# Four edits to a fused graph-Mamba-and-experts kernel: another DMA queue, larger clearing pieces, other PSUM banks, another spread of products

## The reference

```python
x = x + gnn(layernorm(x), adj)            # graph step, then a Mamba block
x = x + ffn(layernorm(x))                 # 8 experts, the best one per token

# gnn:
h = layernorm(relu(adj @ x @ gcn_w + gcn_b)) * ln_g + ln_b
xc, z = h @ w_in                          # 256 + 256
u = silu(conv4(xc)); dt = softplus((u @ w_xp)[:8] @ w_dt + b_dt); B, C = (u @ w_xp)[8:]
state_t = exp(dt * A) * state_(t-1) + dt * B_t * u_t      # 16 states per channel, over all tokens
y = (state_t . C_t + u * D) * silu(z);  out = y @ w_out
# ffn:
H = gelu(x @ W1 + b1);  p = softmax(H @ Wg + bg);  e = argmax(p)
out = p[e] * (H @ Wd[e] + bd[e])
```

## Time and profile before

| | |
|---|---|
| time of three runs, us | 1833.7, 1842.24, 1849.21; median 1842.24 |
| the profiled execution, us | 1857.62 |
| its span from first to last instruction, us | 1855.8 |
| busy, us (share of the span) | TensorE 1534.2 (83%), VectorE 1535.7 (83%), ScalarE 877.1 (47%), GpSimd 874.5 (47%) |
| mean granted TensorE clock | 0.902 of 2.4 GHz |
| DMA | 479.42 MB, mean 258 GB/s; SyncE's queue holds 16 engines 70.7% of the span |

### The profile page before, as it was taken

The page is one execution under the profiler, slowest core; times in us unless marked ns, Lnnn a source line. Parts: engine busy times, 40 slices in busy tenths (PEclk is TensorE's granted clock), DMA queues, the critical chain, the costliest instruction groups (busy, mean ns, idle before and its releaser), DMA issues. The chain is left out here.

```text
span 1855.8 us, 16772 instructions
## 1 busy us (share of the span) xinstructions
PE 1534.2 (83%) x4572; PEld 763.5 (41%) x4572; DVE 1535.7 (83%) x2015; ACT 877.1 (47%) x1558; POOL 874.5 (47%) x466
## 2 busy tenths in 40 slices
PE   6998888887989989898989888998989793633676
PEld 2433343333434545354544444443535341422444
DVE  8058898797899998989899989889999988898621
ACT  3134363452636464554646373646465554634311
POOL 0013333444345464645555554646464645557721
PEclk9999998999998999989999989899999996655788
DMA  8788999999897887879697868688787864333320
GB/s 306 252 299 308 307 337 306 338 317 324 305 329 264 307 294 262 282 255 317 246 322 257 311 233 309 248 307 286 283 299 266 309 215 170 101 124 136 120 70 12
DMA packets 164640, 479.42 MB, mean 258 GB/s; under 512 B 19780, under 2 KB 50512, under 8 KB 164418
## 3 DMA queue, kind: packets, MB, share of 16 engines
q1 hardware_dynamic: 155074, 453.31, 70.7%
q0 software_dynamic: 8320, 20.86, 3.5%
q10 hardware_dynamic: 1152, 4.19, 0.6%
HBM read 448.20 MB, written 33.22 MB: 259 GB/s over the span
## 5 line engine op out<-in xcount | busy, mean ns | idle before, releaser
L1162 PE MATMUL ps_adj<-ring,nodes 128*128 128x512 f32 x2048 | 957.6, 616 | 89.4 <-DMA ring<-adj 66.3
L496 POOL TENSOR_TENSOR h_c<-hidden,bc_ring 128x1024 f32<-128x1024 f32 x256 | 601.0, 2348 | 866.4 <-DVE inject L1030 603.2
L957 DVE TENSOR_TENSOR_SCAN hidden<-decay,state,inject 128x512 f32<-128x512 f32 x512 | 627.6, 1268 | 79.5 <-ACT decay L585 54.1
L1162 PEld LDWEIGHTS ps_adj<-ring,nodes 128*128 128x128 f32 x2048 | 397.0, 198 | 612.0 <-issue 480.2
L1030 DVE TENSOR_TENSOR inject<-dtu_sb,bc_ring 128x1024 f32<-128x1024 f32 x256 | 314.6, 1229 | 55.3 <-DMA bc_ring<-bc_dram 35.1
L585 ACT ACTIVATE decay<-dt_sb,negA 128x512 f32<-128x512 f32 x512 | 340.1, 714 | 8.8 <-DVE dt_sb L984 8.6
L1000 DVE TENSOR_TENSOR y_sum<-y_sum,h_c 128x1024 f32<-128x1024 f32 x224 | 273.8, 1222 | 23.9 <-POOL h_c L496 20.8
L578 ACT COPY state<-hidden 128x2 f32<-128x2 f32 x255 | 49.3, 193 | 473.3 <-DVE hidden L957 471.0
L460 POOL DMA_INDIRECT out<-o_sb,out_at x68 | 92.0, 1354 | 71.6 <-DVE o_sb L862 58.7
L455 POOL DMA_INDIRECT bins<-rec,dest x60 | 87.3, 1455 | 10.8 <-issue 10.2
L450 POOL DMA_INDIRECT got<-bins,row_at x60 | 85.0, 1416 | 14.6 <-issue 11.5
(11 more groups left out here) (201 smaller groups left out, 1387.0 us busy)
## 6 DMA issues: line engine op xcount, KB each, us to landing
ring<-adj SPq DMA_DIRECT2D x512, 512.0 KB
bc_ring<-bc_dram SPq DMA_DIRECT2D x256, 512.0 KB, 5.8
wd_ring<-wd_rows SPq DMA_DIRECT2D x64, 320.0 KB
bins<-nodes SPq DMA_DIRECT2D x128, 129.0 KB, 7.8
nodes<-x_rows ACTq DMA_DIRECT2D x8, 512.0 KB, 12.2
x_tile<-x_rows SPq DMA_DIRECT2D x16, 256.0 KB
wd_rows<-Wd SPq DMA_DIRECT2D x8, 256.0 KB
ring<-Wd SPq DMA_DIRECT2D x1, 2048.0 KB, 7.5
```

The source lines that it names most:

```text
L496: nc.gpsimd.tensor_tensor(h_c[:, s % 2], hidden[:, s % 2], over_halves(bc_ring[:, s % BC_RING, 1]), ALU.mult).then_inc(hc_ready, 1)
L957: scan = nc.vector.tensor_tensor_scan(hidden[:, s % 2, h], decay[:, s % 2, h], inject[:, h], state[:, h, s:s + 1], ALU.mult, ALU.add)
L1162: last = nc.tensor.matmul(ps_adj[:, 0], nodes[:, m], ring[:, g % RING, m % GROUP], start=(m == 0), stop=(m == J - 1))
```

## The change

Four parts. (1) The store of the B and C rows and their loads go from SyncE to ScalarE: the store right behind the copy in slot f[9], the loads at the end of each slot, for the state two slots ahead. (2) The bins are cleared in 32 pieces of 4128 bytes on each of 128 partitions instead of 128 pieces of 1032. (3) The W1 products go to both banks of `ps_e`, `ps_y` and bank 1 of `ps_f`, and GELU takes the `ps_f` bank first; the front's waits for GELU change with it. (4) From body 3 on, as far as `MAIN` has no row, the 32 groups of a tile are spread over the slots by `SHARE` instead of two in each.

```diff
+EVEN = (2,) * SLOTS
+SHARE = (3, 3, 2, 3, 2, 2, 2, 1, 2, 2, 0, 3, 2, 3, 0, 2)
+MAIN = {-2: EVEN, -1: (0, 1, 1, 0, 0, 1, 0, 0, 5, 1, 0, 1, 1, 1, 1, 0),
...
-    FILLS = SPACE // P
-    AREAS = 4
+    AREAS, PARTS = 4, 8
...
-            return (ps_f[:, 0], ps_f[:, 1], ps_y[:, 0], ps_e[:, 0])[k]
+            return (ps_e[:, 0], ps_e[:, 1], ps_y[:, 0], ps_f[:, 1])[k]
...
-                counts = table.get(i, () if table is LEAD else (2,) * SLOTS)
+                counts = table.get(i, () if table is LEAD else SHARE)
...
             def clear_bins(n):
-                sp.dma_start(bins.ap()[n * P:(n + 1) * P], nodes[:].rearrange("p j d -> p (j d)")[:, 0:REC]
-                             ).then_inc(zero_in[n * AREAS // FILLS], 16)
+                area, part = n // PARTS, n % PARTS
+                size = SPACE // AREAS
+                width = size * REC // P // PARTS
+                cells_of = bins.ap()[area * size:(area + 1) * size].rearrange("(p n) c -> p (n c)", p=P)
+                sp.dma_start(cells_of[:, part * width:(part + 1) * width],
+                             nodes[:].rearrange("p j d -> p (j d)")[:, 0:width]).then_inc(zero_in[area], 16)
...
                     if i in (1, 2, 3):
-                        for n in range(3 * (SLOTS * (i - 1) + s), min(3 * (SLOTS * (i - 1) + s + 1), FILLS)):
+                        k = SLOTS * (i - 1) + s
+                        for n in range(AREAS * PARTS * k // (3 * SLOTS), AREAS * PARTS * (k + 1) // (3 * SLOTS)):
                             clear_bins(n)
...
-                    if s == min(f[9] + 2, SLOTS - 1) and front:
-                        sp.dma_start(bc_dram.ap()[q].rearrange("s h n -> h s n"), rows_sb[:]
-                                     ).wait_op(rows_ready, c.value(rows_ready, 1, 1), "sem-ge").then_inc(rows_out, 16)
-                    for d, t in next_state(s, mamba, front):
-
-                        freed = c.value(hc_ready, d, t - BC_RING + 1)
-                        if t == 0:
-                            c.wait(rows_out, d, 16)
-                        dma = sp.dma_start(bc_ring[:, t % BC_RING],
-                                           bc_dram.ap()[p if d == 0 else q, t:t + 1].broadcast_to([P, 2, T]))
...
         @block.scalar
+                def fetch_rows(s):
+                    for d, t in ((0, s + 2), (1, s + 2 - SLOTS)):
+                        if (mamba if d == 0 else front) and 0 <= t < SLOTS:
+                            if t == 0:
+                                c.wait(rows_out, d, 16)
+                            c.wait(hc_ready, d, t - BC_RING + 1)
+                            act.dma_start(bc_ring[:, t % BC_RING],
+                                          bc_dram.ap()[p if d == 0 else q, t:t + 1].broadcast_to([P, 2, T])
+                                          ).then_inc(bc_in[t % BC_RING], 16)
...
-                        for k in range(4):
-                            c.wait(h_done, -1, k + 1)
+                        c.wait(h_done, -1, 4)
+                        for k in (3, 0, 1, 2):
                             nc.scalar.activation(H[:, k], h_bank(k), ACT.Gelu, bias=vec("b1", k)
...
+                        c.wait(rows_ready, 1, 1)
+                        act.dma_start(bc_dram.ap()[q].rearrange("s h n -> h s n"), rows_sb[:]).then_inc(rows_out, 16)
...
                     if not (s in (8, 11, 13) or fast and s == 5):
                         exp_decay(s)
+                    fetch_rows(s)
...
         @block.tensor
                         c.wait(xt_ready, -1, 1)
-                        c.wait(xz_ready, 1 if front else 0, 4 if front else 0)
                         c.wait(bh_ready, -5, 4)
+                        c.wait(o_ready, -5, PICKS + 1)
                         for k in range(4):
+                            if k == 3:
+                                c.wait(xz_ready, 1 if front else 0, 4 if front else 0)
                             product(h_bank(k), [(w1_sb[:, k], xn_cols)]).then_inc(h_done, 1)
                     if front and s == f[8]:
                         c.wait(u_ready, 1, 1)
-                        if ffn:
-                            c.wait(h_ready, -1, 1)
...
                         c.wait(low_ready, 1, 1)
                         if ffn:
-                            c.wait(h_ready, -1, 2)
+                            c.wait(h_ready, -1, 1)
```

More of the change, by code:

```diff
@@ L18 @@
 OUT_SLOTS = (0, 10, 11, 12)
-MAIN = {-1: (0, 1, 1, 0, 0, 1, 0, 0, 5, 1, 0, 1, 1, 1, 1, 0),
+EVEN = (2,) * SLOTS
+SHARE = (3, 3, 2, 3, 2, 2, 2, 1, 2, 2, 0, 3, 2, 3, 0, 2)
+MAIN = {-2: EVEN, -1: (0, 1, 1, 0, 0, 1, 0, 0, 5, 1, 0, 1, 1, 1, 1, 0),
         0: (0, 0, 0, 0, 0, 0, 1, 2, 2, 2, 3, 2, 2, 3, 3, 3),
@@ L371, in body @@
                 q = 1 - p
-                f = FRONT.get(i, range(SLOTS))
                 if i == TILES - 2:
@@ L396, in body @@
                         load_experts(wd_ring[:, p], p, wd_in[p])
-                    if s == min(f[9] + 2, SLOTS - 1) and front:
-                        sp.dma_start(bc_dram.ap()[q].rearrange("s h n -> h s n"), rows_sb[:]
-                                     ).wait_op(rows_ready, c.value(rows_ready, 1, 1), "sem-ge").then_inc(rows_out, 16)
-                    for d, t in next_state(s, mamba, front):
-                        freed = c.value(hc_ready, d, t - BC_RING + 1)
-                        if t == 0:
-                            c.wait(rows_out, d, 16)
-                        dma = sp.dma_start(bc_ring[:, t % BC_RING],
-                                           bc_dram.ap()[p if d == 0 else q, t:t + 1].broadcast_to([P, 2, T]))
-                        if freed is not None:
-                            dma.wait_op(hc_ready, freed, "sem-ge")
-                        dma.then_inc(bc_in[t % BC_RING], 16)
                     if s == SLOTS - 1 and mamba:
@@ L472, in body @@
                         if i - 2 < AREAS:
-                            pool.wait_ge(zero_in[i - 2], 16 * FILLS // AREAS)
+                            pool.wait_ge(zero_in[i - 2], 16 * PARTS)
                         c.wait(dest_step, -2, 6)
@@ L479, in body @@
                         for n in range(AREAS):
-                            pool.wait_ge(zero_in[n], 16 * FILLS // AREAS)
+                            pool.wait_ge(zero_in[n], 16 * PARTS)
                         c.wait(ctrl_step, -4, 13)
```

## The result

The changed kernel takes 1833.97 us, the median of 12 runs (1819.1 to 1843.5), against 1844.02 us for the kernel before in the same rounds. The ratio is 0.994, with a 95% interval of 0.9913 to 0.9968: a gain of about 0.6%, where 1.5% was forecast. The profiled execution took 1837.63 us.

What follows compares the result with a forecast made beforehand. VectorE's idle waits were taken as what can be won, VectorE and TensorE having little room. Terms of -8 (tiles 4 to 13), -15 (tiles 0 to 3) and -4 (tile 14) sum to -27 us: ratio 0.985, 1815 us, range 1775 to 1858.

Steps and rivals of the forecast that it cites:

- Tiles 4 to 13, -8 us: New VectorE waits of 3.2 us a tile replace 4.0 at slot 13: -0.8 us in each of ten tiles.
- the row of state 10: VectorE's wait for slot 10's B row, issued 3.5 us ahead: L - 3.5, so 1.2 us a tile.
- the row of state 13: VectorE's wait for slot 13's B row: L - 3.9 + d, so 2.0 us a tile.
- The decay behind that row: Slot 13's decay on ScalarE would end before `inject` is over; still being last would show the forecast wrong.
- d: In tiles 4 to 13, how late the batch's hidden products reach ScalarE's slot 11: taken as 1.2 us, between 0 and 4.4.
- L: Time from issue to landing of a row load on ScalarE's queue: taken as 4.7 us, between 3.6 and 5.7.
- Rival 1: The other queue makes no difference: L stays 5.7, 5.2 us of waits a tile, 1839 us; chance 0.20.
- Rival 2: TensorE stays at 1.2 GHz from `low_sb` on and L is 5.7: 8.4 us a tile, 1871 us; chance 0.15.
- Rival 4: Batch products come no earlier; slot 13's scan starts at 913.5 instead of 910.5; 1853 us; chance 0.06.
- Tiles 0 to 3, -15 us: Larger pieces save 4 us each in tiles 1 and 2, 3 in tile 3; tile 0 saves 4.
- Tile 14, -4 us: The 3.9 us wait for a B row behind the `Wd` load on the same queue goes; at worst 0.
- The banks at nothing: Moving the W1 products removes TensorE's 3.49 us wait for GELU at slot 8, but by itself gives the end nothing.

Runs made afterwards that it cites:

- second profile: The kernel before, unchanged, run again for another profile: 1847.4 us, ratio 1.0008; that profiled execution took 1845.8 us.
- x_fill: The changed kernel with four products of no use (3.6 us at full clock) added in slot 10 before the second `dt` product: 1839.8 us, ratio 0.9969.
- u_queue: The changed kernel with the store and loads of the B/C rows back on SyncE: 1878.0 us, ratio 1.0194.
- u_pieces: The changed kernel with the bins cleared in 128 small pieces again: 1842.7 us, ratio 0.9982.
- u_banks: The changed kernel with the four W1 products in their old banks, with the old waits for GELU: 1836.9 us, ratio 0.9962.
- u_share: The changed kernel with two adjacency groups in every slot again: 1849.2 us, ratio 1.0036.
- the swap alone: The changed kernel with the batch's hidden products 0 and 1 ahead of the logits in slot 10 on TensorE: 1829.4 us, ratio 0.9899.
- the early loads alone: The changed kernel with rows loaded at the slot's head, not its end, in slots 8, 11 and 13: 1839.3 us, ratio 0.9942.
- the three together: The changed kernel with hidden products before slot 10's logits, row loads at the head of slots 8, 11, 13, and two groups per slot: 1815.4 us, 0.9822.

## Why the prediction was off

The time lies in the range, and tiles 1 to 3 and 14 gave what they were to give or more; but the gain is 10 us by the medians, where the sum had 27. The profile after is 20 us below the first profile and 8 us below the second. Of the 17 us that are missing, 10 lie in the base (last below), 5 in tiles 4 to 13 and 3 in the start; the other tiles gave 1 us more than forecast.

*Tiles 4 to 13, -8 us: the step that failed.* The sum was 3.2 us of new waits a tile against 4.0. The new waits are 3.7; the old ones were 3.5 by the second profile. Of the sum's terms, the row of state 10 costs nothing where 1.2 was forecast, and the row of state 13 costs 1.7 where it was 2.0. The decay behind that row, which the prediction had ending in time, costs 0.75 (that it is still last was a sign of being wrong), and the rows of states 15, 14 and 11, which were not in the sum, 1.3.

The term that was mis-sized is d, by which the batch's products come too late. It was taken as 1.2 us, with 4.4 named for the case that the whole stretch runs at 1.2 GHz. It is ScalarE's wait in slot 11: 5.44 us in tile 7 and 4.2 in the mean of nine tiles. In tile 7 the whole stretch from the transposes on is at 1.2 GHz, which costs about 4 us (`x_fill`), and the wait for the gathered rows `got`, 1.14 us, which the prediction did not see, comes on top. The row of tile 14 had shown what an empty stretch does to the logits; I applied it to the logits and to one product, not to what stands before and behind them.

Two other terms erred the other way and hid part of this. L was taken as 4.7 us; from issue to `inject` at state 13 it is 3.4 to 3.9 in the eight tiles that wait for this row, 3.6 in the mean (888.19 to 891.78 in tile 7). That is not the queue's doing. In these tiles the last adjacency load goes out 15 to 20 us before the row, because TensorE frees no place in the ring, and the DMA engines are nearly idle (a share of 0.10 at the most in the two us before the row). In tile 7 (DMA share and GB/s last):

```profile
886.20:888.20 2.00, 2.00 (x4) 0.93 (x3) 1.93 (x3) 1.66 (x2) 1.83 (x2) 0.50 0.00 0
```

So the 3.6 us are those of SyncE's loads with little beside them. Where adjacency is under way, a load on ScalarE's queue takes no less time than one on SyncE's. State 15's rows in tile 7, on SyncE, ScalarE (the first of the two issues) and VectorE:

```profile
890.47 10.63 SPq L383 DMA_DIRECT2D ring<-adj  x6
...
899.06 0.89 ACTq L588 DMA_DIRECT2D bc_ring<-bc_dram  x2
...
904.75 1.23 DVE L1036 TENSOR_TENSOR inject<-dtu_sb,bc_ring 128x1024 f32<-128x1024 f32 x1 [0.68 <-DMA bc_ring<-bc_dram]
```

These are 5.7 us, and 5.1 to 7.0 in the seven tiles that wait there (up to 8.0 at states 11 and 14), against 4.5 to 6.5 on SyncE's queue before. The prediction cited the Trainium skill (page "DMA: Bandwidth & Descriptors", section "Issuing engines are not separate DMA queues"), by which a second issuer saves issue time alone; from that it worked out that L would stay at 5.7. Beside adjacency the trace agrees with it. What the other queue had cost in `u_queue` is not the transfer either, but SyncE's order of issue, 16.15 us between two adjacency loads. The Trainium skill's second sentence, from the same page, on turns between queues, had been read as speaking for a smaller L; no run shows a smaller L beside adjacency, and the 3.6 does not test it.

And ScalarE's issue runs ahead of its arithmetic: state 10's load was issued while the slot's GELUs still ran,

```profile
866.02 0.33 ACTq L588 DMA_DIRECT2D bc_ring<-bc_dram  x1
...
868.45 1.28 ACT L664 ACT_TABLE_LOAD   x1
```

3.7 us before the slot's last instruction ended (869.73), so state 10 waits for nothing (forecast 1.2 us). At state 13 the issue is 2.2 us ahead. With the measured terms of tile 7, 3.6 - 3.9 + 5.4 - 2.2 = 2.9 us, against 3.10 in the trace; with d at its mean of 4.2 and the rest as in tile 7, 1.7, the mean that was measured. With d at 1.2 there would be no wait at state 13 at all.

*Rival 1* gave 1839, the time nearest to the 1834 measured. What it says of the queue holds, as the loads of state 15 show, but its sum does not: it had 5.2 us of new waits a tile, at states 10 and 13. That its time is close is luck. *Rival 2* named the mechanism that decided, the low clock from `low_sb` on, and priced it with an L of 5.7, which would have made the kernel slower. With the L of 3.6 that the idle engines gave, it only ate the gain. *Rival 4* (products no earlier, the low clock taking all) is nearest to what happened (ScalarE's wait was 41.9 us before and is 37.4 now); it had the row land 4.7 us behind the end of slot 11, where the trace has 1.4 (891.78 against 890.38), and so came out slower.

*Tiles 0 to 3, -15 us.* Tiles 1 to 3 gave 17.1 against the first profile and 14.0 against the second, where 11 was forecast, and `u_pieces` puts 13.3 of that down to the pieces. By the profiles, then, more of the price per MB was in the short rows than the half that I took. Tile 0 was to give 4 and gave nothing: most of its waits in front of `inject` went, but VectorE then waits 12.4 us once for the decay of state 7 (its scan starts at 160.51), because ScalarE stands 13.98 us in front of a copy out of `ps_adj`. So the adjacency of tile 1 seems to set this tile's end whichever wait shows it; no run tests that. And the start lost 3.2 us that the prediction had left out. ScalarE issues the first row behind its work on `dt` (107.51), SyncE had issued it at 104.54:

```profile
112.97 1.23 DVE L1036 TENSOR_TENSOR inject<-dtu_sb,bc_ring 128x1024 f32<-128x1024 f32 x1 [1.95 <-DMA bc_ring<-bc_dram]
```

1.95 us are this wait, the other 1.3 are `dt_sb`, which comes 1.3 us later itself.

*Tile 14, -4 us.* It gave 4.7, but by another way. A row still costs 2.9 us there, and 0.8 the decay; before there were two waits in this tile, 3.9 for the row and 4.4 for the decay, and the prediction had read only the first.

*The banks at nothing* held (`u_banks`), though the wait that took the place of GELU's is mostly the one for `u_sb`, not for `low_sb`.

*The base.* The sum was made against one execution, which lies 13.6 us (0.7%) above the median of the 12 runs; the profile after lies 3.7 above its own. These 10 us are in the 20 between the two profiles, but not in the medians. Such an execution has waits in it that others have not: 40.4 us at state 13 in one profile, 34.7 in the other. That is 6 us, most of the gain forecast for tiles 4 to 13. Against the second profile these tiles gained nothing (996.4 after 992.0).

What stays open: why the logits of the kernel before reach 5.8 us in one to three of the ten tiles, and in which tiles `u_share` loses its 1% in the median, which its one profile, faster than that of the changed kernel, does not show.

## What to carry to other kernels

When work is moved out of a stretch on TensorE to make it shorter, ask what is left there: here, small products and waits alone ran at half the clock and took back part of what the move had won. A late producer delays all that stands behind its consumer on an in-order engine, loads as well as arithmetic, so look for the order in which the producer serves its consumers before moving the loads. Removing a wait pays only if all that stands behind the same cause goes with it: the changed kernel is at 0.994; with the swap alone it is at 0.990, with the early loads alone at 0.994, with the even spread alone at 1.004, and with the three together at 0.982. And before a sum is made against one profile, compare its time with the median of the runs.

## What the hardware showed that was not expected

- A DMA issue on ScalarE does not wait for the arithmetic ahead of it to end: 3.7 us ahead at slot 8's end, 2.2 at slot 11's. It was not seen to pass an instruction that waits for another engine: in tile 7 it came at 888.19, after the wait that ended at 886.52.
- The issue of a row load on ScalarE's queue takes 0.33 us in tiles 4 to 13, where the loads of `nodes` had 0.50 at the start.
- The same load on the same queue took 3.4 to 3.9 us with the DMA engines nearly idle before it (state 13) and 5.1 to 7.0 beside adjacency loads (state 15).
- TensorE's clock was still 0.50 for the products of 128 x 512 behind the slow logits (884.50 to 888.00), and 0.94 in the nine us after that, in which 20 adjacency products ran.
